# Second biases as three-row matmuls on TensorE, larger groups of logits, and a reordered start in a routed layer on one core

## The reference, cut to what matters

```
def reference(x, Wq, Wk, Wv, Wo, gate_w, gate_b, w1, b1, w2, b2):
    xn = layernorm(x)                                  # x is (8, 256, 128)
    Q, K, V = xn @ Wq, xn @ Wk, xn @ Wv                # 16 heads of 8
    Qf, Kf = elu(Q) + 1, elu(K) + 1                    # by head
    num = Qf @ (Kf.T @ V); den = Qf @ sum(Kf) + 1e-6   # by head and batch
    att = (num / den) @ Wo
    probs = softmax(xn @ gate_w.T + gate_b)            # 8 experts
    vals, idx = top_k(probs, 2)
    h = relu(xn @ w1[e] + b1[e])                       # 128 -> 256
    y = h @ w2[e] + b2[e]                              # 256 -> 128
    return x + att + sum over the two experts of vals * y
```

## Time and profile before

| | us |
|---|---|
| median of three runs | 119.73 (119.38 to 120.27) |
| the profiled execution, its own time | 119.96 |
| its span in the profile | 118.2 |
| TensorE busy | 100.9 (85%) |
| VectorE busy | 71.0 (60%) |
| ScalarE busy | 58.4 (49%) |
| GpSimd busy | 50.8 (43%) |

### The profile page before, as it was taken

The page is one execution under the profiler, slowest core; times in us unless marked ns, Lnnn a source line. Parts: engine busy times, 40 slices in busy tenths (PEclk is TensorE's granted clock), DMA queues, the critical chain, the costliest instruction groups (busy, mean ns, idle before and its releaser), DMA issues.

```text
span 118.2 us, 3075 instructions
## 1 busy us (share of the span) xinstructions
PE 100.9 (85%) x763; PEld 91.3 (77%) x763; DVE 71.0 (60%) x291; ACT 58.4 (49%) x167; POOL 50.8 (43%) x66
## 2 busy tenths in 40 slices
PE   6967989999797897579999999999999899999100
PEld 6935968667676786469999999999999799999100
DVE  0749897998718976320575656557566565574600
ACT  1556996454020111117667676667666476666000
POOL 5004800467777778011001404022514458787870
PEclk9999999999999999967999999999999999999955
DMA  3999000002112116999855655856677758882522
GB/s 94 237 322 392 32 0 6 0 0 72 51 48 72 48 53 153 240 246 377 240 129 134 148 140 152 181 143 133 177 176 153 171 107 185 177 152 22 44 22 25
DMA packets 16656, 15.52 MB, mean 131 GB/s; under 512 B 1920, under 2 KB 16256, under 8 KB 16512
## 3 DMA queue, kind: packets, MB, share of 16 engines
q1 hardware_dynamic: 13248, 12.88, 38.8%
q0 software_dynamic: 2816, 2.18, 11.8%
q10 hardware_dynamic: 576, 0.27, 0.9%
HBM read 12.09 MB, written 3.23 MB: 130 GB/s over the span
## 4 chain that ended last, share of the span: by engine, by line
issue 28%; POOL 19%; PE 19%; DVE 13%; DMA 10%; ACT 2%; SPq 2%; POOLq 2%; DVEq 0%
POOL out L459 19%; DMA x_tok<-in_x 6%; DMA out<-res 5%; PE banks L968 4%; PE banks L937 3%; PE banks L1030 3%; PE banks L990 3%; PE banks L1005 2%; DVE att L766 2%; POOLq L115 2%; DVE rden L762 1%; SPq L354 1%; PE banks L921 1%; DVE idx L634 1%; PE banks L967 1%
## 5 line engine op out<-in xcount | busy, mean ns | idle before, releaser
L547 ACT ACTIVATE h<-banks,w_now 128x128 f32<-128x128 f32 x118 | 36.9, 364 | 19.7 <-PE banks L1061 19.7
L459 POOL DMA_INDIRECT out<-acc,token x16 | 25.0, 1562 | 34.5 <-DVE acc L795 33.3
L1061 PE MATMUL banks<-xsT,w_now 128*128 x236 | 37.5, 283 | 0.1
L1074 PE MATMUL banks<-w_all,h 128*128 x236 | 36.2, 277 | 0.3 <-DVE y L787 0.2
L1061 PEld LDWEIGHTS banks<-xsT,w_now 128*128 128x128 f32 x236 | 31.9, 197 | 0.8 <-issue 0.5
L787 DVE TENSOR_TENSOR y<-banks,w_all 128x128 f32<-128x128 f32 x59 | 17.2, 292 | 24.1 <-PE banks L1074 15.6
L1074 PEld LDWEIGHTS banks<-w_all,h 128*128 128x128 f32 x236 | 30.9, 192 | 1.0 <-issue 0.9
L795 DVE SCALAR_TENSOR_TENSOR acc<-y,xs,acc 128x128 f32 x59 | 20.7, 351 | 0.8 <-DVE y L787 0.5
L444 POOL DMA_INDIRECT sorted_dram<-xrow,slot x16 | 15.8, 990 | 5.3 <-issue 4.6
L893 PE MATMUL banks<-ones 128*128 128x128 f32 x42 | 7.9, 355 | 1.1 <-POOL ones L387 1.1
L893 PEld LDWEIGHTS banks<-ones 128*128 128x128 f32 x42 | 7.4, 265 | 1.5 <-POOL ones L387 1.1
(11 more groups left out here) (97 smaller groups left out, 108.7 us busy)
## 6 DMA issues: line engine op xcount, KB each, us to landing
w_now<-in_w1b SPq DMA_DIRECT2D x59, 129.0 KB, 2.5
w_all<-in_w SPq DMA_DIRECT2D x1, 1536.0 KB, 9.6
out<-res SPq DMA_DIRECT2D x4, 256.0 KB, 5.4
xs<-sorted_dram SPq DMA_DIRECT2D x3, 276.0 KB, 5.4
x_tok<-in_x SPq DMA_DIRECT2D x3, 256.0 KB, 6.6
xs<-sorted_dram SPq DMA_DIRECT2D x2, 138.0 KB, 3.4
x_tok<-in_x SPq DMA_DIRECT2D x2, 128.0 KB, 2.6
sorted_dram<-xrow,slot POOLq DMA_INDIRECT x16, 2.4
```

The lines of the kernel that those rows point to most:

```text
L459: nc.gpsimd.indirect_dma_start(out=out_rows, out_offset=bass.IndirectOffsetOnAxis(ap=token[:, s:s + 1], axis=0), in_=acc[:, s * D:(s + 1) ...
L547: nc.scalar.activation(h[:, i % NH, c, :], h_ps[i % NHP][:, c * P:(c + 1) * P], ACT.Relu, bias=w1_now[:, i % NW, H + c:H + c + 1]).then_in ...
L1061: last = nc.tensor.matmul(h_ps[i % NHP][:, c * P:(c + 1) * P], w1_now[:, i % NW, c * P:(c + 1) * P], xsT[:, bass.ds(toff, P)], start=True, ...
L1074: last = nc.tensor.matmul(y_ps[i % NYP], h[:, i % NH, c, :], w2_all[:, bass.ds(woff + c * D, D)], start=(c == 0), stop=(c == KC - 1))
```

## The change

- *Second bias.* b2 is loaded a second time as 8 rows. GpSimd splits it into three bf16 parts (`split_b2`, five small steps whose sum is the f32 value), and three DMAs lay them as three rows of `b2_split`, an expert's 128 values at its offset. `second_product` opens each sum with a matmul of three rows of ones and the three rows of the expert. `take_y` is called no more; `accumulate` reads PSUM, and the buffers of the products come free by `acc_done`.
- *Start.* `wq` and the gate's bias move from ScalarE's queue to SyncE's, behind x and the constants.
- *Groups.* `take_logits` takes four tiles; pairs are found for groups of 8, 4 and 4 tiles; `choose`, `shares`, `shift`, `gate_values` take eight. The banks of PSUM and the calls on TensorE are moved to fit.
- *Order.* `finish_k(0)` and `finish_k(1)` go behind the first `places`; `divide(0)` goes ahead of `mask_kv(3)`; `residual(1)` ahead of `divide(3)`.
- *Fillers.* One `warm_up` of three becomes two; eight more stand behind the last `project_out`, ahead of the first `transpose_rows`, and wait for the third residual.

The core of the diff:

```diff
+    EARLY, LATE = slice(0, 8), slice(8, T)
+    PAIR_GROUPS = [(0, 8), (8, 12), (12, 16)]
...
-        vg_ps = [banks[:, (2, 3, 4, 6)[b % 4], 0:R * (D + E)].rearrange("p (r n) -> p r n", r=R) for b in range(B)]
-        k_ps = [banks[:, i, :].rearrange("p (t d) -> p t d", t=4) for i in (7, 1, 0, 7)]
+        vg_four = [banks[:, i:i + 2, 0:R * (D + E)].rearrange("p b (r n) -> p b r n", r=R) for i in (2, 6, 2, 6)]
+        k_ps = [banks[:, i, :].rearrange("p (t d) -> p t d", t=4) for i in (4, 1, 0, 7)]
...
+        def bias_by_pe(i):
+
+            return True
...
             sp.dma_start(cst[:], consts).then_inc(consts_in, 16)
+            sp.dma_start(gate_bias[:], gate_b.partition_broadcast(P)).then_inc(gate_b_in, 16)
+            sp.dma_start(wq_f[:], wq).then_inc(wq_in, 16)
             sp.dma_start(wo_f[:], wo).then_inc(wo_in, 16)
+            sp.dma_start(b2_f[:], b2).then_inc(b2_in, 16)
             sp.dma_start(w2_all[:], w2).then_inc(w2_in, 16)
+            sp.wait_ge(b2_step, 5)
+            for j in range(3):
+                sp.dma_start(b2_split[j:j + 1, :].rearrange("o (e c) -> o e c", c=WROW)[:, :, 0:D],
+                             b2_parts[j][:]).then_inc(b2_placed, 16)
...
+            def split_b2():
+
+                pool.wait_ge(b2_in, 16)
+                nc.gpsimd.tensor_copy(b2_parts[0][:], b2_f[:]).then_inc(b2_step, 1)
+                pool.wait_ge(b2_step, 1)
+                nc.gpsimd.tensor_tensor(b2_rest[:], b2_f[:], b2_parts[0][:], ALU.subtract).then_inc(b2_step, 1)
...
             fill_rows()
-            shift(0)
-            shift(1)
-            gate_values(0)
-            gate_values(1)
+            split_b2()
+            shift()
+            gate_values()
...
-            nc.scalar.dma_start(wq_f[:], wq).then_inc(wq_in, 16)
-            nc.scalar.dma_start(gate_bias[:], gate_b.partition_broadcast(P)).then_inc(gate_b_in, 16)
...
             def accumulate(i, toff, goff):
-                dve.wait_ge(y_done, i + 1)
+                if bias_by_pe(i):
+                    dve.wait_ge(l2_done, i + 1)
+                    share = y_ps[i % NYP]
+                else:
+                    dve.wait_ge(y_done, biases_by_dve(i + 1))
+                    share = y[:, i % 2, :]
                 mine = acc[:, bass.ds(toff, D)]
...
             late_shift()
-            finish_k(0)
             pair_starts()
             places(1, slice(0, 4))
+            finish_k(0)
+            finish_k(1)
             places(2, slice(4, T))
-            finish_k(1)
             mask_kv(0)
...
             finish_q(2)
+            divide(0)
             mask_kv(3)
             finish_q(3)
-            divide(0)
             divide(1)
...
             keep_table()
+            residual(1)
             divide(3)
-            residual(1)
             residual(2)
...
+                elif bias_by_pe(i - NYP):
+                    pe.wait_ge(acc_done, i - NYP + 1)
                 else:
-                    pe.wait_ge(y_done, i - NYP + 1)
+                    pe.wait_ge(y_done, biases_by_dve(i - NYP + 1))
+                if bias_by_pe(i):
+                    pe.wait_ge(b2_placed, 16 * 3)
+                    nc.tensor.matmul(y_ps[i % NYP], ones_bf[0:3, 0:P], b2_split[:, bass.ds(woff, D)],
+                                     start=True, stop=False)
                 for c in range(KC):
                     last = nc.tensor.matmul(y_ps[i % NYP], h[:, i % NH, c, :],
                                             w2_all[:, bass.ds(woff + c * D, D)],
-                                            start=(c == 0), stop=(c == KC - 1))
+                                            start=(c == 0 and not bias_by_pe(i)), stop=(c == KC - 1))
...
             project_k(0)
             transpose_x(2)
-            warm_up(3)
+            warm_up(2)
             project_vg(2)
+            project_vg(3)
             transpose_x(3)
-            project_vg(3)
+            project_vg(4)
             transpose_x(4)
+            project_vg(5)
             rank_rows(0)
-            project_vg(4)
-            rank_rows(1)
-            project_vg(5)
             project_vg(6)
             project_vg(7)
+            rank_rows(1)
             project_k(1)
+            project_q(0)
             rank_rows(2)
-            project_q(0)
-            rank_rows(3)
...
             pe.wait_ge(w2_in, 16)
+            warm_up(8, residuals=3)
             transpose_rows(0)
```

More of the change, by code:

```diff
@@ L129, in linear_attention_with_pair_sorted_experts @@
         wo_f = sb("wo_f", [P, D])
+        b2_f = sb("b2_f", [E, D])
+        b2_rest = sb("b2_rest", [E, D])
+        b2_parts = [sb(f"b2_part{j}", [E, D], BF16) for j in range(3)]
+        b2_split = sb("b2_split", [3, E * WROW], BF16)
         gate_bias = sb("gate_bias", [P, E])
@@ L324, in normalised, with biases_by_dve, pairs_known @@
             return [sum(len(n) for n in norm[:i + 1]) for norm in (NORM_DVE, NORM_ACT, NORM_POOL)]
+        def bias_by_pe(i):
+            return True
+        def biases_by_dve(i):
+            return sum(not bias_by_pe(j) for j in range(i))
+        def pairs_known(t):
+            return sum(t >= a for a, _ in PAIR_GROUPS)
         def group_of_visit(i):
@@ L569, in _ @@
             exp_gates(0)
-            exp_gates(1)
             exp_k(0)
-            for b in range(4, 7):
+            for b in range(4, 6):
                 copy_v(b)
             exp_k(1)
+            copy_v(6)
             copy_v(7)
             exp_q(0)
+            exp_gates(1)
             exp_k(2)
-            exp_gates(2)
             exp_q(1)
@@ L794, in accumulate @@
                     dve.wait_ge(acc_done, i)
-                nc.vector.scalar_tensor_tensor(out=mine, in0=y[:, i % 2, :], scalar=xs[:, bass.ds(goff, 1)], in1=mine,
+                nc.vector.scalar_tensor_tensor(out=mine, in0=share, scalar=xs[:, bass.ds(goff, 1)], in1=mine,
                                                op0=ALU.mult, op1=ALU.add).then_inc(acc_done, 1)
@@ L872, in _ @@
                     copy_xsT(3)
-                if i == 0:
+                if i == 0 and not bias_by_pe(0):
                     take_y(0, woffs[0][0])
-                if i + 1 < NI:
+                if i + 1 < NI and not bias_by_pe(i + 1):
                     take_y(i + 1, woffs[(i + 1) // LOADS][(i + 1) % LOADS])
@@ L887, in _, with warm_up @@
         def _(pe):
-            def warm_up(times, after=0):
+            def warm_up(times, after=0, residuals=0):
                 pe.wait_ge(ones_set, 1)
@@ L920, in project_vg @@
                 for r in range(R):
-                    last = nc.tensor.matmul(vg_ps[b][:, r, :], xT[:, (R * b + r) * P:(R * b + r + 1) * P],
+                    last = nc.tensor.matmul(vg_four[b // 2][:, b % 2, r, :], xT[:, (R * b + r) * P:(R * b + r + 1) * P],
                                             wkvg_f[:, D:KVG], start=True, stop=True)
@@ L949, in rank_rows @@
                 pe.wait_ge(pair_done, g + 1)
-                nc.tensor.matmul(rank_ps[:, blk_tiles(g), :], before_bf[:], of_pair[:, blk_tiles(g), :],
-                                 start=False, stop=False)
-                for t in range(4 * g, 4 * g + 4):
+                a, b = PAIR_GROUPS[g]
+                nc.tensor.matmul(rank_ps[:, a:b, :], before_bf[:], of_pair[:, a:b, :], start=False, stop=False)
+                for t in range(a, b):
                     last = nc.tensor.matmul(rank_ps[:, t + 1:T + 1, :], ones_bf[:, 0:P],
```

154 lines of the change are left out of this document (78 added, 76 removed).

## The result

The change makes the kernel slower: 134.28 us (134.05 to 134.44) beside 119.56 for the kernel before on the same chip, ratio 1.124, interval 1.115 to 1.132. The prediction was 135.7 with a range of 125 to 139. The profiled execution after has a span of 132.6 us (118.2 before) and took 134.44.

What follows compares the result with a forecast made beforehand. TensorE bounds the visits, at eight records and 0.89 us each. From 119.96 us: +21.2 bias, -2.6 end, -1.2 standing still, -1.5 start, less 0.2 for the median, gives 135.7 us; range 125 to 139.

Steps and rivals of the forecast that it cites:

- The bias costs 0.36 us: Visits: each three-row bias matmul on TensorE pays 0.31 us for changing row count plus 0.05; 59 add 21.2 us.
- VectorE's delay at the end: After the last visit: accumulation reads PSUM directly and follows the last matmul, 0.8 us in place of 3.4, -2.6 us.
- TensorE's standing still: Visits: half of TensorE's 2.5 us idle time goes at the slower pace, -1.2 us (0 to -2.5).
- The start, -1.5 us: Ahead of the visits: earlier slots and a held clock together save 1.5 us (+0.5 to -3).
- The price of the half clock: At the rows: 16 records took 0.213 us each at half clock; at 0.111 they take 1.6 us less.
- what is gained is the clock: At the rows: fillers keep full clock, saving 1.6 us, while the rows are transposed 0.2 us later.
- the path of the rows: Ahead of the visits: slots 0.6 us earlier, so scatters and row loads both move by -0.8 us (-0.3 to -1.5).
- The small steps that split b2: GpSimd, start: five steps of 0.3 us lie in its 6.0 us wait; uncovered, they would delay the first scatter 1.5 us.
- Rival B: Visits: three rows run like 128, 0.055 us a bias, 3.2 in all; whole 117.6 or 119.1 us; chance 0.13.
- the point that decides: Whole kernel: gains are 5.3 us, so the change is faster if one bias costs under 0.09 us.

Runs made afterwards that it cites:

- the start edits: Changed kernel with the second biases back on VectorE, b2 still split and placed but unread: 117.83 us, ratio 0.991 to the kernel before.

## Why the prediction was right, point by point

- *The bias costs 0.36 us because of the step between row counts.* Right, size and reason: 1.246 us a visit from start to start of the second products, 1.25 predicted. Shown by three runs: the same matmul on 128 rows costs 0.11, a second few-row matmul 0.055, and 64 rows as much as three. What exactly happens inside the engine is not seen; that both weight loads are uncovered is (and the idle times of 0.12 and 0.07 us above).
- *VectorE's delay at the end, -2.6 us.* 3.4 became 1.1, so -2.3: the last scatter still waits for the one before it.
- *TensorE's standing still, -1.2 us.* This is the term that was mis-sized. From the first second-product record to the last are 54.9 to 109.6 before and 53.7 to 126.3 after, 54.7 and 72.6 us. 58 biases at 0.357 are 20.7; the difference is 17.9, so 2.8 us of waiting are gone, all of it and not half, and a little more than the range of 0 to -2.5 allowed. At 1.25 us a visit nothing that TensorE waited for is late any more, and at the 1.00 us of the experiment with 128 rows hardly anything is (53.8 of 54.0 us busy there). The 1.6 us too few here, less the 0.3 too many at the end, are most of the 1.4 by which the forecast lies above the measured time.
- *The start, -1.5 us.* Right in size (0.991, -1.4 us beside the kernel before), by luck in part. The price of the half clock was read rightly from the earlier trace rows, but that it comes in every execution was assumed, and one more profile has it at 1.00. Two steps failed. The first is "what is gained is the clock": the start edits gain 1.1 us among executions with a high mean clock too, and about as much without the fillers as with them. The second is the path of the rows, which were made to follow the scatters. The first slots did come earlier than forecast (-1.7 against -0.8: VectorE starts on the fourth part of x at 7.59 instead of 8.73 in this profile, though the kernel before itself moved by 0.8 between two profiles), but the row loads hang on the table of visits and SyncE's six weights (-0.9), and the fillers took what was left. Against the second profile of the kernel before (first scatter at 23.79, row loads at 46.53, first product at 51.15) this start gains 0.9 and 0.15 us, and its first product is later. Which part of the start brings the 1.1 us stays open. The small steps that split b2 stayed covered: GpSimd still waited 4.8 us for VectorE before its first gates.
- *Rival B, the cheap bias.* Its price of 0.055 us was wrong even for 128 rows, and with it the chance of a gain: at 0.11 us a bias is above the 0.09 that was worked out as the point that decides, and that kernel is in fact slower, by 1.5%.

## What to carry to other kernels

A small matmul placed between large ones can be priced by the step between row counts and not by its columns (0.30 and 0.055 us here): look in the trace for the nearest case of a change in the number of rows and read the start of the true stream on either side. If a few rows must be added to a sum on the engine that sets the pace, fill them with zeros to the row count of their neighbours (0.11 instead of 0.36 us, here still 1.5% slower than no such matmul), or let them follow one another (the second cost 0.055; that all in one place pay the step once was not tried). And a half clock in one profile need not come in the next execution: a second profile of the same kernel, before anything is built on it, would have shown that, and the mean clock of every execution how often.

## What the runs showed of the hardware that was not expected

- A bf16 matmul of 128 columns on 128 rows among f32 ones costs 0.11 us and not 0.055. That the f32 weights that follow load for about 0.10 us, and that the shorter stream covers only part of them, is a reading of their starts that no run tested.
- A bias on 64 rows costs as much as one on three: 394 records in 54 us with either.
- The granted clock fell to half behind an idle time of 1.06 us in one execution, and stayed at full speed over 1.08 and 1.24 us in two others, the second of them of the same kernel.
- Indirect scatters with addition follow one another at 1.87 us on GpSimd; near the end, where about every second visit frees a tile, two visits of 0.9 us are no longer than that, and in the kernels with the start edits the queue of scatters sets the end from about 98 us on.
